# Attention on one core: a third PSUM bank for turned probabilities, and the products by V gathered into every fourth unit

## The reference, cut to what matters

```python
qkv = (x @ Wqkv + bqkv).reshape(B, L, 3, n_heads, head_dim)
scores = jnp.einsum('bqhd,bkhd->bhqk', q, k) / math.sqrt(head_dim)
scores = scores + slopes[None, :, None, None] * bias[None, None]
probs = jax.nn.softmax(scores, axis=-1)
out = jnp.einsum('bhqk,bkhd->bqhd', probs, v).reshape(B, L, D)
```

## Time and profile before

| | |
|---|---|
| Median of 3 runs | 3427.95 us (3424.53 to 3428.9) |
| Time of the profiled execution | 3425.09 us |
| Its span | 3423.5 us |
| Granted TensorE clock over the span | 0.972 of full speed |
| PE / DVE / ACT / POOL busy | 3140.5 / 2344.2 / 1824.1 / 1072.7 us |
| First scores to last product by V in `attend` | 356.6 to 1474.4 us |

### The profile page before, as it was taken

How to read it: one execution, slowest core, us unless ns; L and a number is a source line. 1 busy time by engine, 2 the same in 40 slices (tenths; PEclk the granted TensorE clock), 3 DMA queues, 4 the chain that set the end, 5 groups by cost and what they waited for, 6 DMA issues and landing times. The chain is left out here.

```text
span 3423.5 us, 56908 instructions
## 1 busy us (share of the span) xinstructions
PE 3140.5 (92%) x19209; PEld 2277.0 (67%) x19234; DVE 2344.2 (68%) x4173; ACT 1824.1 (53%) x3126; POOL 1072.7 (31%) x949
## 2 busy tenths in 40 slices
PE   6999799999999999969999699989999999958887
PEld 5777566666666666647777577768888888724443
DVE  5563788888888888854454489975444444599996
ACT  3342788888888888822222322232222222249995
POOL 3343422232222322234433346541110111015666
PEclk9999999999999999989999899999999999989999
DMA  6775322122212221255653644441111011311112
GB/s 211 242 244 175 105 63 61 58 86 70 62 58 77 74 64 58 96 177 193 213 178 128 210 124 135 131 152 51 42 44 43 25 39 31 98 39 50 62 50 74
DMA packets 239350, 350.52 MB, mean 102 GB/s; under 512 B 31792, under 2 KB 129104, under 8 KB 239184
## 3 DMA queue, kind: packets, MB, share of 16 engines
q1 hardware_dynamic: 208256, 290.41, 26.3%
q0 software_dynamic: 8912, 32.82, 2.9%
q10 hardware_dynamic: 22016, 25.17, 2.1%
HBM read 210.68 MB, written 137.64 MB: 102 GB/s over the span
## 5 line engine op out<-in xcount | busy, mean ns | idle before, releaser
L887 DVE CUSTOM_DVE_ANT_0 attend_scores<-attend_scores,attend_bias_table 128x1024 f32<-128x1024 f32 x512 | 630.2, 1231 | 164.1 <-PE attend_scores L741 160.8
L814 ACT ACTIVATE attend_probs<-attend_scores,attend_neg_max 128x1024 f32<-128x1024 f32 x512 | 571.6, 1116 | 140.3 <-DVE attend_neg_max L887 130.6
L753 PE MATMUL attend_turned<-ident,attend_probs 128*128 128x128 f32 x4096 | 556.5, 275 | 12.5 <-DVE attend_probsT L895 12.4
L753 PEld LDWEIGHTS attend_turned<-ident,attend_probs 128*128 128x128 f32 x4096 | 472.0, 140 | 121.2 <-DVE attend_probsT L895 30.8
L741 PE MATMUL attend_scores<-attend_k_stack,attend_q_stack 96*128 96x512 f32 x1024 | 372.8, 446 | 17.7 <-DMA attend_q_stack<-qk_parts 14.6
L822 ACT COPY attend_probsT<-attend_turned 128x512 f32<-128x512 f32 x640 | 359.6, 583 | 24.1 <-PE attend_turned L753 22.5
L2244 DVE TENSOR_TENSOR cross_ffn_h_lo<-cross_ffn_hidden,cross_ffn_h_hi 128x512 fp32r<-128x512 f32 x128 | 104.3, 821 | 339.4 <-ACT cross_ffn_h_hi L2135 338.8
L768 PE MATMUL attend_out_acc<-attend_probsT,attend_v_in 128*32 128x256 f32 x4096 | 312.9, 389 | 0.7 <-DVE attend_out_full L905 0.7
L703 POOL TENSOR_TENSOR attend_out_parts<-attend_out_full,attend_out_parts 128x256 fp32r<-128x256 f32 x64 | 46.5, 726 | 846.1 <-ACT attend_out_parts L829 846.1
L741 PEld LDWEIGHTS attend_scores<-attend_k_stack,attend_q_stack 96*128 96x128 f32 x1024 | 153.9, 189 | 175.1 <-issue 157.5
L895 DVE COPY attend_probsT<-attend_turned 128x512 f32<-128x512 f32 x384 | 263.4, 686 | 1.0 <-PE attend_turned L753 1.0
(11 more groups left out here) (296 smaller groups left out, 6674.0 us busy)
## 6 DMA issues: line engine op xcount, KB each, us to landing
qk_parts<-qkv_qk_out SPq DMA_DIRECT2D x64, 512.0 KB, 3.2
attend_k_stack<-qk_parts SPq DMA_DIRECT2D x192, 128.0 KB, 2.5
attend_q_stack<-qk_parts SPq DMA_DIRECT2D x192, 128.0 KB, 2.7
qkv_wq_raw<-L_ffn_w POOLq DMA_DIRECT2D x16, 1024.0 KB, 7.6
o_parts<-attend_out_parts ACTq DMA_DIRECT2D x64, 256.0 KB, 2.5
carried_o_in<-o_parts SPq DMA_DIRECT2D x32, 512.0 KB, 6.3
qkv_x_in<-x SPq DMA_DIRECT2D x8, 1024.0 KB, 5.6
v_rows<-qkv_v_out SPq DMA_DIRECT2D x32, 256.0 KB, 3.4
```

The source lines that it names most:

```text
L753: last = pe.transpose(turned[:, x, c], probs[:, i % 2, k * P:(k + 1) * P], ident[:, :])
L814: act.activation(probs[:, i % 2], scores[:, i % 2], ACT.Exp, bias=neg_max[:, i % 4:i % 4 + 1], scale=-1.0, accum_out=den[:, qg % 2, j, h:h ...
L887: dve.tensor_tensor_reduce(scores[:, i % 2], scores[:, i % 2], bias_table[:, h, at:at + T], -1.0, BIG, ALU.add, ALU.min, neg_max[:, i % 4: ...
```

## The change

`turned` gets a third bank, which takes the place of the bank of `den_turned`. The halves of the units go through the three banks in rotation (half m of a group to bank m mod 3, with one place left out after unit 3 for the denominators). The denominators are turned into that place, and copied out by ACT in unit 4 instead of unit 5. Semaphores that count copies and turns are kept per bank instead of per half, with counts computed by `earlier`. The products by V are issued four chunks at a time, chunks 0 to 3 in unit 3 and 4 to 7 in unit 7, behind the transposes of that unit. The denominators' transposes stay in unit 3, behind the four chunks.

```diff
-        turned = ps("turned", [P, 2, HB, P])
+        turned = ps("turned", [P, 3, HB, P])
         out_acc = ps("out_acc", [P, 2 * QG])
-        den_turned = ps("den_turned", [P, 2 * QG])
...
+        DEN_UNIT = 3
+        halves = [(k, x) for k in range(PER_GROUP) for x in range(2)]
+        bank_of = {(k, x): (2 * k + x + (k > DEN_UNIT)) % 3 for k, x in halves}
+        den_bank = (2 * DEN_UNIT + 2) % 3
+        order_of = {half: sum(bank_of[h] == bank_of[half] for h in halves[:m]) for m, half in enumerate(halves)}
+        per_bank = [sum(bank_of[half] == bank for half in halves) for bank in range(3)]
...
+        def earlier(turn, i, x):
+
+            half = (i % PER_GROUP, x)
+            return (turn * G + i // PER_GROUP) * per_bank[bank_of[half]] + order_of[half]
...
                     for x in range(2):
-                        if not (isinstance(u, int) and u == 0):
-                            pe.wait_ge(copied[x], u)
+                        half = (i % PER_GROUP, x)
+                        bank, done = bank_of[half], earlier(turn, i, x)
+                        if not (isinstance(done, int) and done == 0):
+                            pe.wait_ge(copied[bank], done)
+                        if half == after_den and exists(turn, i // PER_GROUP, 1):
+                            pe.wait_ge(rdenT_ready, turn * G + i // PER_GROUP)
                         for c in range(HB):
                             k = x * HB + c
-                            last = pe.transpose(turned[:, x, c], probs[:, i % 2, k * P:(k + 1) * P], ident[:, :])
-                        last.then_inc(turned_ready[x], 1)
+                            last = pe.transpose(turned[:, bank, c], probs[:, i % 2, k * P:(k + 1) * P], ident[:, :])
+                        last.then_inc(turned_ready[bank], 1)
...
                     if exists(turn, qg, 1):
-                        if k > 0:
-                            times_v(turn, qg, k - 1)
-                        if k == PER_GROUP - 1:
-                            times_v(turn, qg, k)
-                        if k == 3:
+                        if k % 4 == 3:
+                            for c in range(k - 3, k + 1):
+                                times_v(turn, qg, c)
+                        if k == DEN_UNIT:
                             turn_den(turn, qg)
...
-                    if k == 5 and exists(turn, qg, 1):
+                    if k == DEN_UNIT + 1 and exists(turn, qg, 1):
                         copy_den(turn, qg)
```

More of the change, by code:

```diff
@@ L596, in attend @@
         probs_ready = sem("probs_ready")
-        turned_ready = [sem(f"turned_ready{x}") for x in range(2)]
-        copied = [sem(f"copied{x}") for x in range(2)]
+        turned_ready = [sem(f"turned_ready{bank}") for bank in range(3)]
+        copied = [sem(f"copied{bank}") for bank in range(3)]
         pv_step = sem("pv_step")
@@ L623, in shifted @@
             return (turn + (i + by) // UNITS, (i + by) % UNITS) if not 0 <= i + by < UNITS else (turn, i + by)
+        DEN_UNIT = 3
[4 more added lines that the diff above has]
+        per_bank = [sum(bank_of[half] == bank for half in halves) for bank in range(3)]
+        before_den = max(half for half in halves if bank_of[half] == den_bank and half[0] <= DEN_UNIT)
+        after_den = min(half for half in halves if bank_of[half] == den_bank and half[0] > DEN_UNIT)
+        def earlier(turn, i, x):
+            half = (i % PER_GROUP, x)
+            return (turn * G + i // PER_GROUP) * per_bank[bank_of[half]] + order_of[half]
         def exists(turn, group, back):
@@ L759, in times_v @@
                     if c == 0:
-                        for x in range(2):
-                            pe.wait_ge(copied[x], (group + 1) * PER_GROUP)
+                        for bank in range(3):
+                            pe.wait_ge(copied[bank], (group + 1) * per_bank[bank])
                         if not (isinstance(group, int) and group == 0):
@@ L774, in turn_den @@
                     pe.wait_ge(wide_ready, group + 1)
+                    if isinstance(turn, int) and turn == TURNS:
+                        pe.wait_ge(copied[den_bank], TURNS * G * per_bank[den_bank])
+                    else:
+                        pe.wait_ge(copied[den_bank], earlier(turn, qg * PER_GROUP + before_den[0], before_den[1]) + 1)
                     for j in range(JT):
-                        last = pe.transpose(den_turned[:, j * P:(j + 1) * P],
+                        last = pe.transpose(turned[:, den_bank, j],
                                             rden_wide[:, j].rearrange("p h d -> p (h d)"), ident[:, :])
@@ L810, in exp @@
                     if not (isinstance(u, int) and u < 2):
-                        act.wait_ge(turned_ready[1], u - 1)
+                        t, k = shifted(turn, i, -2)
+                        act.wait_ge(turned_ready[bank_of[k % PER_GROUP, 1]], earlier(t, k, 1) + 1)
                     if i % PER_GROUP == 0 and exists(turn, qg, 2):
@@ L818, in copy @@
                     qg, h, j = split(i)
-                    act.wait_ge(turned_ready[x], turn * UNITS + i + 1)
+                    bank = bank_of[i % PER_GROUP, x]
+                    act.wait_ge(turned_ready[bank], earlier(turn, i, x) + 1)
                     if i % PER_GROUP == 0 and exists(turn, qg, 2):
                         act.wait_ge(pv_step, (turn * G + qg - 1) * TB)
-                    act.copy(probsT[:, qg % 2, x * HB:(x + 1) * HB, h, j * P:(j + 1) * P], turned[:, x]).then_inc(copied[x], 1)
+                    act.copy(probsT[:, qg % 2, x * HB:(x + 1) * HB, h, j * P:(j + 1) * P], turned[:, bank])\
+                       .then_inc(copied[bank], 1)
                 def round_out(turn, qg):
@@ L839, in copy_den @@
                     act.wait_ge(den_turned_ready, turn * G + qg)
[L841 removed]
+                    act.copy(rdenT[:, :].rearrange("p (j q) -> p j q", j=JT), turned[:, den_bank, 0:JT]).then_inc(rdenT_ready, 1)
                 def before(turn, i):
@@ L891, in copy @@
                     qg, h, j = split(i)
-                    dve.wait_ge(turned_ready[1], turn * UNITS + i + 1)
+                    bank = bank_of[i % PER_GROUP, 1]
+                    dve.wait_ge(turned_ready[bank], earlier(turn, i, 1) + 1)
                     if i % PER_GROUP == 0 and exists(turn, qg, 2):
                         dve.wait_ge(pv_step, (turn * G + qg - 1) * TB)
-                    dve.tensor_copy(probsT[:, qg % 2, HB:TB, h, j * P:(j + 1) * P], turned[:, 1]).then_inc(copied[1], 1)
+                    dve.tensor_copy(probsT[:, qg % 2, HB:TB, h, j * P:(j + 1) * P], turned[:, bank])\
+                       .then_inc(copied[bank], 1)
                 def before(turn, i):
```

## The result

The changed kernel takes 3479.18 us (median of 4 runs, 3475.24 to 3482.43). The kernel before took 3426.24 us in the same comparison. The ratio is 1.0156 (95% interval 1.0143 to 1.0169), so the change costs 53 us. The forecast was 3487 us, 59 us slower than the kernel before.

A forecast was written before the change was run, and what follows sets the result against it. PE's queue was all but full, but long steps would make the two-buffer score chain the bound: +0.93 us in each of 63 groups is 59 us, added to the 3427.95 us median for 3487 us; range 3455 to 3520 us.

The forecast's parts named there:

- its walk: Start-time chain through one group from unit 3's scores: 18.29 us against 17.36, +0.93 us a group; chance 0.58 as it stands.
- The mechanism: Two score buffers: during a long product step DVE and ACT get nothing new, so a 2 us PE stop is not covered.
- the circle of exp and scores: Score buffer's loop, exp to scores to maximum to exp: 1.26 + 0.93 + 1.33 = 3.52 us for two units.
- PE's work decides: Rival: PE stays the bound, 2.13 us less per group, about 3294 us; chance 0.07, anything faster included.
- The price of a step: Four chunks on PE in units 3 and 7: next work starts 0.57 + 3 x 0.435 = 1.87 us later.
- the denominators' copy: ACT, before exp 5: copy starts 0.48 us behind its transposes, exp 5 0.45 us later, at 4.34.
- The 1.74 us between two exps: On ACT, two exps with one copy between them; puts exp 6 at 4.34 + 1.74 = 6.08.
- the register instructions for the counts: Per-bank semaphore counts before waits on PE, ACT, DVE: costed at nothing; a quarter microsecond per group (16 us) left in range.
- The denominators don't hold ACT up: Rival: exp 5 starts once its maximum and ACT allow; group 0.25 us shorter, +0.68 us, 3471 us; chance 0.15.
- The rule on pulled weight loads: PE pulls loads ahead of matmuls: 0.41 us behind steps would vanish, 17.47 us a group, 7 us more; trace judged to disagree.
- up to 0.60 us of waits in PE's sum: Third bank lets a unit's transposes start before DVE's copy of the unit ahead; can save up to 0.60 us a group.
- a fall in the new gaps: PE's granted clock was expected to stay at 1.00; a fall in the new gaps would cost more than anything else.

The follow-up runs named there:

- the pairs: Changed kernel, denominators ahead of products in unit 3, two chunks each in units 1, 3, 5, 7: 3383.57 us; same steps in the two-bank kernel before: 3452.52 us.
- the five steps: Three banks, denominators ahead of products, chunks 2, 1, 2, 1, 2 in units 1, 2, 4, 6, 7: 3357.26 us; kernel before with these steps: 3407.74 us.
- the step of eight: Changed kernel with all eight chunks in one step in unit 7, denominators in unit 3: 3503.81 us, ratio 1.0228.

## Why the prediction was right, and where its walk was off

- **The mechanism held.** The scores behind a long step come late, and the circle of exp and scores does not catch up. It was shown by the long steps alone (+54 us without the bank) and by the series of steps with three banks, which contradicts "PE's work decides" from the pairs on.
- **The sum.** The group was forecast at 18.29 us and is 18.21; +0.93 us a group was forecast and +0.85 measured. The distances were forecast as 3.6, 2.0, 1.7, 1.8, 3.4, 1.4 and twice 2.2 and are 3.59, 1.81, 1.67, 1.91, 3.40, 1.37, 2.14, 2.32. The price of a step (32 records in one piece) is right: the next work starts 1.86 us behind the start of the step, 1.87 forecast. That the group is right to 0.08 us is in part luck, since two terms were mis-sized in opposite directions.
- **The first mis-sized term, too long,** is the denominators' copy. It starts 0.48 us behind the transposes as said (1040.69 to 1041.17), but exp 5 follows 0.27 us later instead of 0.45, before the copy has ended. So exp 5 starts at 4.14 in the walk's time instead of 4.34, and the scores in unit 5 at 5.40 instead of 5.60, 1.26 behind it as priced. The pace behind it, for exp 6, was misread too, though exp 6 is not on the chain that sets the group. The 1.74 us between two exps were taken for ACT's pace. But in the rows of before the second of them starts 1.32 us behind its maximum (1023.08 to 1024.40), so it was waiting for DVE. ACT alone can follow faster, by the rows of the last section, and exp 6 starts at 5.81, where the circle lets it (4.48 + 1.33), instead of 6.08.
- **The second mis-sized term, put at nothing,** is the register instructions for the counts. I had argued from the kernel before, where two exps are 1.74 us apart in the looped turns and in the first. There exp starts 1.33 us behind its maximum nearly everywhere. In the looped turns of the changed kernel that distance is 1.40 us in units 3, 4 and 7 and 1.45 in unit 0. In its last turn, which like the first is written out with constant counts, it is 1.32 us in the same units. Unit 3, in a looped turn and in the last one:

```profile
1034.63 1.23 DVE L910 CUSTOM_DVE_ANT_0 attend_scores<-attend_scores,attend_bias_table 128x1024 f32<-128x1024 f32 x1
1036.04 1.11 ACT L835 ACTIVATE attend_probs<-attend_scores,attend_neg_max 128x1024 f32<-128x1024 f32 x1 [0.64 <-DVE attend_neg_max L910]
...
1489.65 1.23 DVE L910 CUSTOM_DVE_ANT_0 attend_scores<-attend_scores,attend_bias_table 128x1024 f32<-128x1024 f32 x1
1490.97 1.11 ACT L835 ACTIVATE attend_probs<-attend_scores,attend_neg_max 128x1024 f32<-128x1024 f32 x1 [0.50 <-DVE attend_neg_max L910]
```

  By the trace ACT runs 18 register instructions in a looped group of the changed kernel and 10 in one of the kernel before, and none in the last turn. Two of these handovers, exp 7 and exp 3, are links of the walk's chain. With 0.20 us less at exp 5, 0.06 more at exp 7, 0.01 less at the step in unit 7 and 0.07 more at exp 3 the walk gives 18.21, which is what was measured. The group of the last turn takes 18.00 us (17.28 in the kernel before, where a looped one takes 17.35). The loop thus costs 0.22 us a group in the changed kernel and 0.07 in the kernel before. If the difference is put down to the added register instructions, they cost 0.15 us in each of the 56 groups of the 14 looped turns, 8 of the 53 us by this estimate.
- **A rival nearly without weight.** "The denominators don't hold ACT up" priced their place at 0.25 us a group, and moving it gave 0.05. The price was reckoned from exp 5 at 4.34. As exp 5 starts at 4.14 already, 0.20 of it was never there.
- **The rule on pulled weight loads** did not shorten the steps. The gap of 0.41 us in front of the work behind a step is there after each of the two steps. The Trainium skill, page "TensorE: Matmul & The Clock Gate", section "The mechanism", sets a condition: the load must not meet the row groups of the matmuls in flight, or must go to a background buffer. The product steps use all 128 rows and the scores 96 of them, so the first half of the condition is not met here, and the prediction used the rule more widely than it is stated. Why the gap is there remains open. PE's weight loads in the changed kernel, the columns of the earlier trace rows:

```profile
1040.69 0.20 PEld L797 LDWEIGHTS attend_turned<-ident,attend_rden_wide 128*128 128x128 f32 x2 [0.41 <-issue]
...
1049.68 0.30 PEld L754 LDWEIGHTS attend_scores<-attend_k_stack,attend_q_stack 96*128 96x128 f32 x2 [0.41 <-issue]
```

- **What the prediction did not price** is the third bank by itself. I only gave it up to 0.60 us of waits in PE's sum. It is worth 0.39 us a group with single chunks, 1.06 with pairs, 0.87 with the five steps and nothing with fours.
- **What is left of the waits with the third bank alone** is the 0.21 us between 16.97 and PE's 16.76. It stands in one place: the scores issued in unit 3 come 2.32 us behind those of unit 2 (1041.14 to 1043.46), where one unit with a chunk takes 2.11. They wait for exp 3, 1.26 us behind its start at 1042.20, and exp 3 starts 1.40 us behind its maximum. That is the circle again, behind DVE's reciprocals, and 0.07 us of it are the counts.

## What to carry to other kernels

Where an engine is full, look at how deep the buffers behind it are before gathering its work: gathering saves the change-overs, but each piece must fit into the time that the other engines can live on what is already buffered. Here, with two score buffers in every run, that was one or two chunks, not four, and the pairs did best with single chunks between them. Count the instructions that compute a wait's count as well: on a chain that bounds the loop they cost 0.07 us a handover here. The Trainium skill, page "Perfetto Trace Analysis", section "Matmul Optimizations", advises to let matmuls run back to back in batches, because the engine scales its power with its use. The granted clock was 1.00 in the stage with each kernel here, so no run shows that reason at work. The batches of this case gained by fewer change-overs, up to pairs spread over the group, and lost at fours by the waits around them. And a freed buffer is worth most together with the order that needs it (21.5 us with the old order, 50 us between the two kernels with five steps), so try the two apart and together.

## What the runs showed of the hardware that was not expected

- The pace of ACT is shorter than the rows of before let it seem. With one copy between them, exp 6 of the kernel with five steps starts 1.56 us behind exp 5. Its maximum had started 1.69 us ahead of it, more than the usual 1.33, so it was not waiting for DVE:

```profile
1034.87 1.23 DVE L909 CUSTOM_DVE_ANT_0 attend_scores<-attend_scores,attend_bias_table 128x1024 f32<-128x1024 f32 x1 [0.28 <-PE attend_scores L754]
1035.00 1.15 ACT L834 ACTIVATE attend_probs<-attend_scores,attend_neg_max 128x1024 f32<-128x1024 f32 x1
...
1036.56 1.16 ACT L834 ACTIVATE attend_probs<-attend_scores,attend_neg_max 128x1024 f32<-128x1024 f32 x1
```

- Register instructions show in the time of the engine that waits. In the changed kernel one exp follows another after 1.80 us from unit 7 to unit 0 (1045.02 to 1046.82, by its row below), with 1.45 us behind the maximum. In the last turn, with constant counts, the same pair is 1.74 us apart. In units 2 and 6 the distance from maximum to exp is 1.33 us in the looped turns too.

```profile
1046.82 1.12 ACT L835 ACTIVATE attend_probs<-attend_scores,attend_neg_max 128x1024 f32<-128x1024 f32 x1
```

- The granted clock stayed at 1.00, the upper of its two levels, in every kernel from 400 to 1350 us. The prediction had kept a fall in the new gaps open. The lowest busy share of PE was 87% (829 of 950 us with the step of eight), with waits of up to 0.7 us, as the windows of that run show:

```profile
400.00:1350.00 950.00, 828.68 (x7453) 611.11 (x7452) 724.59 (x1278) 755.22 (x1429) 214.97 (x116) 1.00 0.22 65
```
